# Keys and values kept in one place for the whole program and fetched during the last steps of the front; tile 1's mask and wo fetched in pieces

## What is computed

```python
x = x + relu(segment_sum((norm * (h @ W0))[src], dst) * norm + bias0)   # front
h = relu(layernorm(x))
for l in range(2):
    q, k, v = (h @ Wq[l].T + bq[l]) / 8, h @ Wk[l].T, h @ Wv[l].T       # 8 heads of 64
    scores  = (q[dst] * k[src]).sum(-1)                                 # one per edge and head
    w       = softmax of scores over the edges of one dst
    h = batchnorm(h + segment_sum(w * v[src], dst) @ Wo[l].T + bo[l])
    h = batchnorm(h + relu(h @ W1[l].T + b1[l]) @ W2[l].T + b2[l])
out = x + layernorm(h)
```

## Time and profile before

| | us |
|---|---|
| median of 3 runs | 3460.18 |
| lowest and highest of them | 3458.36, 3462.82 |
| the profiled execution, device time | 3465.55 |
| its span, first to last instruction | 3463.7 |
| front, layer 0's attention from / to | 0 to 991, 991 to about 2000 |
| layer 1's attention from / to | 2328 to about 3320 |

### The profile page before, as it was taken

One profiled execution on the slowest core, in us unless ns is written; L12 is line 12 of the kernel. 1 busy time (PEld: TensorE's weight loads), 2 busy tenths in 40 slices (PEclk: granted clock), 3 DMA queues, 4 the chain that ended last, 5 costly groups with the idle time before them and its releaser, 6 DMA issues. The chain is left out here.

```text
span 3463.7 us, 72225 instructions
## 1 busy us (share of the span) xinstructions
PE 3034.8 (88%) x24802; PEld 2390.4 (69%) x24802; DVE 2354.1 (68%) x6951; ACT 1951.4 (56%) x3918; POOL 2176.8 (63%) x1979
## 2 busy tenths in 40 slices
PE   2360899999947999999999989989999999999985
PEld 2120466666636888888888877767888888888875
DVE  9798344343426888888888854218888888888856
ACT  0120444444426777787877731227777787777734
POOL 2788888888006777777777720007777777777734
PEclk9995999999978999999999999999999999999987
DMA  9544776666379999998999841239999999999951
GB/s 371 81 82 94 148 133 118 125 121 123 97 171 167 166 166 166 175 167 166 168 165 168 154 98 24 48 73 171 165 165 166 169 173 165 164 164 171 153 121 59
DMA packets 1294527, 497.26 MB, mean 144 GB/s; under 512 B 1236806, under 2 KB 1262431, under 8 KB 1285974
## 3 DMA queue, kind: packets, MB, share of 16 engines
q1 hardware_dynamic: 1153262, 460.73, 67.5%
q0 software_dynamic: 133120, 0.80, 4.1%
q10 hardware_dynamic: 7788, 31.21, 2.7%
HBM read 154.06 MB, written 80.99 MB: 68 GB/s over the span
## 5 line engine op out<-in xcount | busy, mean ns | idle before, releaser
L1377 DVE CUSTOM_DVE_ANT_0 prob<-s_ps,mask 125x500 f32<-125x500 f32 x1600 | 1058.3, 673 | 307.6 <-PE s_ps L1224 231.1
L1146 POOL TENSOR_TENSOR staged<-prob,staged 125x500 f16<-125x500 f32 x960 | 1064.5, 1115 | 155.1 <-ACT staged L1140 85.8
L1314 ACT ACTIVATE prob<-prob,neg_max 125x1000 f32<-125x1000 f32 (+1 forms) x960 | 954.7, 994 | 120.7 <-DVE scrap L1383 118.3
L1224 PE MATMUL s_ps<-keys,queries 128*125 128x500 f16 x3200 | 947.2, 378 | 43.0 <-DMA values<-v_heads 25.4
L444 POOL DMA_INDIRECT counts<-count,cell x320 | 678.6, 2121 | 182.9 <-issue 106.8
L1255 PEld LDWEIGHTS o_ps<-values,across 125*125 125x125 f16 x7680 | 592.4, 139 | 223.1 <-issue 49.9
L1255 PE MATMUL o_ps<-values,across 125*125 125x128 f16 x7680 | 608.0, 222 | 60.6 <-DMA across<-staged 60.1
L1140 POOL CAST staged<-prob 125x500 f16<-125x500 f32 x640 | 385.5, 602 | 419.4 <-ACT prob L1314 259.1
L1390 DVE TENSOR_TENSOR p_lo<-t_ps,p_hi 125x500 f16<-125x500 f32 x640 | 431.6, 674 | 95.7 <-ACT p_hi L1324 95.0
L1235 PE MATMUL t_ps<-identity,prob 125*125 125x125 f32 x2560 | 413.2, 284 | 3.5 <-ACT agg L1334 2.9
L1324 ACT CAST p_hi<-t_ps 125x500 f16<-125x500 f32 x640 | 361.1, 564 | 87.4 <-PE t_ps L1235 87.0
(11 more groups left out here) (153 smaller groups left out, 3544.2 us busy)
## 6 DMA issues: line engine op xcount, KB each, us to landing
mask<-bias_rows SPq DMA_DIRECT2D x200, 218.8 KB
counts<-xt ACTq DMA_DIRECT2D x8, 3054.0 KB, 37.3
parts<-counts SPq DMA_DIRECT2D x20, 1093.8 KB
bias_rows<-edge_bias SPq DMA_DIRECT2D x20, 1093.8 KB
queries<-q_tiles SPq DMA_DIRECT2D x80, 250.0 KB, 3.9
pair_row<-pair_flat SPq DMA_DIRECT2D x40, 437.5 KB
across<-staged SPq DMA_TRANSPOSE x960, 3.3
q_tiles<-q_both SPq DMA_DIRECT2D x80, 125.0 KB, 3.1
```

What stands on the lines that cost most here:

```text
L1146: engine.tensor_tensor(here[0:P, BPC:2 * BPC, 0:P], prob[u % PROBS][:, k * KC:(k + 1) * KC].rearrange("p (s c) -> p s c", s=BPC), here[0:P ...
L1224: mm = pe.matmul(s_ps[n % SB][:, 0:KC], lhsT=queries[b][:, h, part, :], rhs=keys[:, h, c * KC:(c + 1) * KC], start=(part == 0), stop=(part ...
L1314: act.activation(here, here, ACT.Exp, bias=neg_max[u % 4][:, :], accum_out=sums[u // H % 2][:, u % H, piece:piece + 1]).then_inc(exped, 1)
L1377: dve.tensor_tensor_reduce(out=prob[u % PROBS][:, at], in0=s_ps[n % SB][:, 0:KC], in1=bias[b][:, at], scale=1.0, scalar=MASKED, op0=ALU.ad ...
```

## The change

**Places.** `keys` and `values` are allocated at the top and live throughout. The front's tiles are views into them: `hw` in `values`; `parts` in heads 0 to 3 and `cnt` in heads 4 to 7 of `keys`; before that `w0_sb`, the one-hot tiles and `below` in `keys`.

**Fetching.** The last two node tiles (STRAIGHT = 2) of keys and values no longer go through DRAM: they are copied from the projection's tiles straight into place. The other 18 (STAGED) are stored as before and fetched back by SP inside the front: heads 0 to 3 of the keys at the end of step t = 20, heads 4 to 7 right after the last mask rows' store in step 21, and all values in step 21, after the last use of `hw`. `load_head` and its waits are gone; PE has one wait on the keys and one on the values in layer 0. SP's last waits in the front cover the straight copies, not the fetches.

**Tile 1's mask, queries and wo.** In both layers they are no longer issued ahead of the transposes. Queries are issued at unit 0, mask chunks at units 1 to 5, `wo` at unit 6, each ahead of that unit's transposes.

```diff
+        keys = sb(top, "keys", [128, H, N], F16)
+        values = sb(top, "values", [P, H, NT, 2 * DH], F16)
...
+    STRAIGHT = 2
+    STAGED = NT - STRAIGHT
...
-        hw = sb(ctx, "hw", [P, NT, D])
+        hw = values[:, :, :, :].rearrange("p h t e -> p (h t e)").bitcast(F32).rearrange("p (t d) -> p t d", t=NT)
+        parts = [keys[0:P, 2 * b:2 * b + 2, :].rearrange("p h n -> p (h n)").bitcast(U16) for b in range(2)]
+        cnt = [keys[0:P, 4 + 2 * b:6 + 2 * b, :].rearrange("p h n -> p (h n)").bitcast(F32) for b in range(2)]
...
+                def keys_back(heads):
+                    for h in heads:
+                        sp.dma_start(keys[:, h, 0:STAGED * P], k_heads[h * 128:(h + 1) * 128, 0:STAGED * P]).then_inc(keys_early, 16)
+
+                def values_back():
+                    for half in range(2):
+                        heads = slice(half * H // 2, (half + 1) * H // 2)
+                        load_rows(sp, values[:, heads, 0:STAGED, :].rearrange("p h t e -> p h (t e)"),
+                                  v_heads.rearrange("(h p) e -> p h e", h=H)[:, heads, 0:STAGED * 2 * DH], values_early)
+
+                def keys_straight(t):
+                    nodes = slice(t * P, (t + 1) * P)
+                    sp.wait_ge(k_low, t + 1)
+                    for part, tile in ((0, k_hi[t % 2]), (1, k_lo[t % 2])):
+                        for odd in range(2):
+                            sp.dma_start(keys[64 * part:64 * part + 64, odd::2, nodes],
+                                         tile[64 * odd:64 * odd + 64, :, :]).then_inc(keys_late, 16)
+
+                def values_straight(t):
+                    sp.wait_ge(v_low, t + 1)
+                    store_rows(sp, values[:, :, t, :], v_both[t % 2][:, :, :], values_late)
...
                     if 0 <= t - 2 < NT:
                         store_bias(t - 2)
+                    if t == NT + 1:
+
+                        keys_back(range(H // 2, H))
                     if t >= 3:
                         store_q(t - 3)
+                    if 3 <= t < NT + 1:
                         store_k(t - 3)
+                    if t >= NT + 1:
+                        keys_straight(t - 3)
+                    if t == NT + 1:
+                        sp.wait_ge(cnt_t_used, NKC * NT)
+                        values_back()
                     if 0 <= t - 2 < NT:
                         store_x1(t - 2)
-                    if t >= 3:
+                    if 3 <= t < NT + 1:
                         store_v(t - 3)
+                    if t >= NT + 1:
+                        values_straight(t - 3)
+                    if t == NT:
+                        for b in range(2):
+                            sp.wait_ge(qkv_stored[b], QKV * STAGED // 2)
+                        sp.wait_ge(merged, NKC * NT)
+                        keys_back(range(H // 2))
...
                 for b in range(2):
                     sp.wait_ge(bias_stored[b], BOTH * NT // 2)
-                    sp.wait_ge(qkv_stored[b], QKV * NT // 2)
+                    sp.wait_ge(qkv_stored[b], QKV * STAGED // 2 + 32)
...
+                sp.wait_ge(keys_late, STRAIGHT * 4 * 16)
+                sp.wait_ge(values_late, STRAIGHT * BOTH)
...
                 load_queries(0)
                 for c in range(NKC):
-                    if layer == 0 and c < 2:
-                        load_head(c)
                     load_mask(0, c)
-                if layer == 0:
-                    for h in range(2, H):
-                        load_head(h)
-                load_queries(1)
-                for c in range(NKC):
-                    load_mask(1, c)
-                sp.dma_start(wo_sb[:, :, :].rearrange("p c d -> p (c d)"), g["wo"][layer * 128:(layer + 1) * 128, :]
-                             ).then_inc(wo_loaded, 16)
                 for u in range(UNITS):
                     t, h = u // H + 1, u % H
-                    if 1 < t < NT:
+                    if t < NT:
 
                         if h == 0:
-                            sp.wait_ge(maxed, U0 + H * (t - 1))
+                            if t > 1:
+                                sp.wait_ge(maxed, U0 + H * (t - 1))
                             load_queries(t)
                         if 0 < h <= NKC:
                             load_mask(t, h - 1)
+                        if t == 1 and h == NKC + 1:
+                            sp.dma_start(wo_sb[:, :, :].rearrange("p c d -> p (c d)"), g["wo"][layer * 128:(layer + 1) * 128, :]
+                                         ).then_inc(wo_loaded, 16)
                     for k in BY_DMA:
                         turn(u, k)
...
-                    if layer == 0 and u < H and c == 0:
-                        pe.wait_ge(heads_loaded[h // 2], 2 * (16 + BOTH))
+                    if layer == 0 and u == 0 and c == 0:
+                        pe.wait_ge(g["keys_early"], H * 16)
...
+                    if layer == 0 and u == 0 and k == 0:
+                        pe.wait_ge(g["values_early"], 2 * BOTH)
```

More of the change, by code:

```diff
@@ L171, in gnn_kernel @@
         vec = sb(top, "vec", [128, 30])
+        keys = sb(top, "keys", [128, H, N], F16)
+        values = sb(top, "values", [P, H, NT, 2 * DH], F16)
+        keys_early, keys_late = sem("keys_early"), sem("keys_late")
+        values_early, values_late = sem("values_early"), sem("values_late")
         front(nc, sem, psum, sb, locals())
@@ L182, in front @@
     vec, q_tiles, k_heads, v_heads = g["vec"], g["q_tiles"], g["k_heads"], g["v_heads"]
+    keys, values = g["keys"], g["values"]
+    keys_early, keys_late, values_early, values_late = g["keys_early"], g["keys_late"], g["values_early"], g["values_late"]
     XR = 4
+    STRAIGHT = 2
+    STAGED = NT - STRAIGHT
     dve_steps, waits_met = g["dve_steps"], g["waits_met"]
@@ L212, in front @@
             x_sb = sb(first, "x_sb", [P, NT, D])
-            w0_sb = sb(first, "w0_sb", [128, FC, D])
+            room = keys[:, :, :].rearrange("p h n -> p (h n)")
+            w0_sb = room[:, 0:2 * FC * D].bitcast(F32).rearrange("p (c d) -> p c d", c=FC)
+            room = room[0:EP, 2 * FC * D:].bitcast(BF16)
+            onehot_hi = [room[:, b * QC * HI:(b + 1) * QC * HI].rearrange("p (c w) -> p c w", w=HI) for b in range(2)]
+            room = room[:, 2 * QC * HI:]
+            onehot_lo = [room[:, b * QC * LO:(b + 1) * QC * LO].rearrange("p (c w) -> p c w", w=LO) for b in range(2)]
+            below = room[:, 2 * QC * LO:2 * QC * LO + TH * NCOL].rearrange("p (t c) -> p t c", t=TH)
             earlier = sb(first, "earlier", [EP, 2 * GE - EP])
@@ L220, in front @@
             ramp = sb(first, "ramp", [EP, LO], BF16)
-            onehot_hi = [sb(first, f"onehot_hi{b}", [EP, QC, HI], BF16) for b in range(2)]
-            onehot_lo = [sb(first, f"onehot_lo{b}", [EP, QC, LO], BF16) for b in range(2)]
             pair = sb(first, "pair", [EP, NCOL])
@@ L235, in front @@
             moved = sb(first, "moved", [EP, BC])
-            below = sb(first, "below", [EP, TH, NCOL], BF16)
             needed = sb(first, "needed", [EP, NT])
@@ L247, in front @@
         with ExitStack() as second:
-            parts = [sb(second, f"parts{b}", [P, ROW], U16) for b in range(2)]
-            cnt = [sb(second, f"cnt{b}", [P, N]) for b in range(2)]
             bias = [sb(second, f"edge_bias{b}", [P, N]) for b in range(2)]
@@ L855, in transformer @@
     with ExitStack() as ctx:
-        keys = sb(ctx, "keys", [128, H, N], F16)
-        values = sb(ctx, "values", [P, H, NT, 2 * DH], F16)
         stats = sb(ctx, "bn_stats", [128, FC, NCH, 6])
-        g = dict(g, keys=keys, values=values, stats=stats,
+        g = dict(g, stats=stats,
                  projected=0, last_gain=sb(ctx, "last_gain", [128, FC]), last_shift=sb(ctx, "last_shift", [128, FC]))
@@ L1071, in attention @@
         wo_loaded = sem("wo_loaded")
-        heads_loaded = [sem(f"heads_loaded{h}") for h in range(H // 2)]
         q_loaded = [sem("q_loaded0"), sem("q_loaded1")]
@@ L1156, in load_queries @@
                                      q_tiles[t * DH:(t + 1) * DH, :]).then_inc(q_loaded[t % 2], 16)
-                def load_head(h):
-                    sp.dma_start(keys[:, h, :], g["k_heads"][h * 128:(h + 1) * 128, :]).then_inc(heads_loaded[h // 2], 16)
-                    load_rows(sp, values[:, h, :, :].rearrange("p t e -> p (t e)"), g["v_heads"][h * P:(h + 1) * P, :], heads_loaded[h // 2])
                 def load_mask(t, c):
```

## The result

The changed kernel takes 3433.18 us (median of 4 runs, 3430.84 to 3436.49) against 3459.49 before (4 runs beside it); the medians are 26.3 us apart, where 30 were forecast. The ratio worked out from the single runs is 0.9930, with a 95% interval of 0.9915 to 0.9944; by it the change saves 24 us, between 19 and 29. The span of the profiled execution is 3434.7 us.

The account below looks back on a forecast made before the run. Layer 0's attention start was taken as bound by bytes queued ahead of the transposes. Terms: -43.2 - 2 + 11 + 4 = -30.2 us, from 3465.55 to 3435.4, less 5.4 to the runs' median: 3430, range 3417 to 3446.

Parts of the forecast that it names:

- 1 and 2: layer 0's start, to unit 3's maximum: Layer 0's attention start: -43.2 us without keys and values, -1 with tile 1's mask and wo not ahead of transposes.
- 3: the front's tail: End of the front: fetching keys and values there delays the start of layer 0's attention by 11 us.
- 4: units 3 to 8, layer 0: First attention tile: tile 1's mask and wo among tile 0's transposes cost +2 us in each layer, bounds 0 and 8.
- 2 and 4: layer 1, start to unit 8: Layer 1's first tile: -1 us at the start, +2 us for mask and wo among the transposes.
- The drain: Front's last steps: 6.91 MB of keys and values at 257 GB/s take 26.9 us, with the last stores and copies queued behind.
- The 358 GB/s of the Trainium skill: HBM limit of one core: by it the fetches take 19.3 us and the front ends 3.4 us later, not 11.
- The first half of the keys: Front, about 946: 2.30 MB need 9.0 us with 15 us of room before the next transfer; cost 0.
- One of my own signs of being wrong: First attention tile: the prediction is wrong if PE waits for transposed chunks by more than 5 us.
- The slower rival: Front: products with hw slow down as DMAs share their region; at 60 ns each, 48 us more, 3478 us; chance 0.03.
- The rival of first tiles bound by DMA: First attention tiles: mask and wo among the transposes cost 8 us in each layer, giving 3442 us; chance 0.12.

Follow-up runs that it names:

- before_again: The kernel before the change, unchanged, run and traced once more; 3460.04 us, ratio to before 1.0007.
- changed_again: The changed kernel, unchanged, run and traced once more; 3438.21 us in a slower group, ratio to before 0.9933.
- masks_ahead: Against the changed kernel: tile 1's queries, mask and wo issued ahead of the first transposes again in both layers; 3434.04 us, ratio to before 0.9917.
- values_128: Against the changed kernel: values held in 128 rows, moved as one transfer instead of two over 112 and 13 partitions; 3424.31 us, ratio to before 0.9907.
- v128_masks_ahead: Against the changed kernel: values in 128 rows, and tile 1's queries, mask and wo ahead of the transposes; 3415.31 us, ratio to before 0.9882.
- the odd trace: First trace of the unchanged kernel before: the loop's first mask store at 380.0, against 382.8 to 385.1 in thirteen traces; its execution took 3465.55 us.

## Why the prediction was right, point by point

The traces of before and before_again, and of changed and changed_again, give each term with its scatter.

| term | forecast | measured |
|---|---|---|
| 1 and 2: layer 0's start, to unit 3's maximum | -44.2 | 73.56, 71.12 to 29.86, 29.75: -42.5 |
| 3: the front's tail | +11 | 29.56, 29.98 to 41.35, 41.52: +11.7 |
| 4: units 3 to 8, layer 0 | +2 | 27.11, 28.36 to 30.95, 31.93: +3.7 |
| 2 and 4: layer 1, start to unit 8 | +1 | 57.89, 57.65 to 59.71, 59.54: +1.9 |
| sum | -30.2 | -25.2 |

The sum of the marks, -25.2, answers to the -26.3 of the medians and the -24 of the ratio. The forecast time was 3.2 us too low; the sums differ by 5.0 us, in four terms that are off by 0.7 to 1.7 us each and all the same way: every gain came out smaller and every cost larger.

- **The bound of layer 0's start was read rightly.** That layer 1's start, in the same trace, shows what is left when keys and values are gone, held to 2 us: the first chunk at +20.11 against layer 1's +20.86. Before's own two traces reach unit 3 at 73.56 and 71.12, so 1.2 us of the term are scatter.
- **The drain came out right by luck: two errors cancel.** I priced keys and values alike at 257 GB/s. The keys move at about 400, and the values in the four windows from 980 to 1000 at a mean of 233: for 2.30 MB and 4.61 MB that is 5.8 and 19.8 us, 25.6 in all, where I had 26.9. The row I took was a mean over both kinds. For keys alone it would have given 9.0 us for 5.8, for values alone 17.9 for 19.8.
- **The 358 GB/s of the Trainium skill** ("DMA: Bandwidth & Descriptors", Specifications, where it is half of what one stack of memory gives to two cores) are no limit for this one-core program: two windows show 402 and 405. The drain took longer than that figure would give, but for another reason than a lower limit, in the main the cut of the values: without it the tail is 33.67 us, 4 more than before the change.
- **The first half of the keys was free, as forecast.** It is issued at 948.87, and the next store goes out at 965.45, 30.92 us after the one before, as in the kernel before.
- **Part 4 was mis-sized.** I took +2 for the tile and -1 for the start in each layer, so by my own sum this part of the change costs more than it gives, and I did not say so. Against before, layer 1 shows +1.9 for both; against masks_ahead it is 1.9 to 3.1 us in each layer, and between values_128 and v128_masks_ahead 4.6 and 2.7. The step that failed is the choice of the lower bound "nearer the waits". A likely reason, which no run tests: the waits of the earlier trace rows are those of a tile in which PE is busy 48.33 us for eight units, against 43.4 at the pace of the bare ones, as it also has the output products of the tile before to do; so the DMA has more time there, and tile 0 has no tile before it. The -1 for the start came out at -0.5 to -0.6 in layer 0 (against layer 1's start of before) and -0.4 in layer 1, at unit 3's maximum, most likely since most of what stood ahead was through before the first transpose was issued.
- **One of my own signs of being wrong was met.** PE waits 5.9 us for transposed chunks in layer 0's first tile (6.8 in changed_again), where I had put more than 5 as a sign that the prediction is wrong, and units 3 to 8 take 30.95 us there, outside the 28 to 30 that I expected; in layer 1 they take 29.95, inside. Both are the mis-sized term 4. The second attention block starts at 1006.80, not near 1002; 3.85 us of that arose before the loop's first store, in the comparison with the odd trace.
- **The slower rival** is excluded: each step of the front's loop but the first takes 30.91 to 30.97 us before and after, and the products with `hw` keep their median of 592 ns in both. The rival of first tiles bound by DMA, which stood at 8 us in each layer, is half true in layer 0, where the term came out at 3.7.

## What to carry to other kernels

In this kernel a transfer's price is its bytes over the rate of its own shape: take the rate from a window in which only that kind moves, and look whether it goes over 128 partitions. What is fetched ahead of time belongs where DMA is idle, and it lengthens a stage when that stage's last stores stand behind it in the queue; pieces placed among tight work cost more than the same bytes in front of it, as long as those are through before the tight work begins. Compare marks within one trace and times within one group of runs, and before a shift of a few microseconds is explained, take a second trace of the old kernel.

## What the hardware showed that I had not expected

- Fetches over 128 partitions with rows of 4500 bytes moved at 402 to 405 GB/s, and with rows of 4608 bytes at 377 to 411; the latter, cut into 112 and 13 partitions, moved at 192 to 278, with DMA's share above 1 in each case. A share near 1 says that the engines are occupied, not that they move as much as they can.
- An issue of two small copies held SP for 14.91 us while the queue was full, and for 5.38 us when half of the values were fetched later. The wait moved with the bytes and showed no cost of its own.
- 160 unused bytes ahead of the front's tiles, which move the start of a 5 MB load off a multiple of 256 bytes, changed nothing that can be measured (1.0010, 0.9999 to 1.0022).
